# The product with V for two key tiles at once in every second step of an attention block

## The chip, the cores and the metric

One core of one Trainium2 chip. The metric is device time in microseconds (us) for one execution of the whole program, lower is better.

## The reference

One transformer block over X of shape 4 x 1024 x 128 (B = 4 batches, L = 1024 tokens, width 128): a modulated layer norm, attention with 16 heads of 64, and a top-2-of-4 expert layer. The change lies in the attention alone:

```python
qkv = X @ W_qkv + b_qkv                      # b l (H 3 DK) -> Q, K, V of each head
scores = jnp.einsum('bhqd,bhkd->bhqk', Q, K) / np.sqrt(DK)
attn = jax.nn.softmax(scores, axis=-1)
out = jnp.einsum('bhqk,bhkv->bhqv', attn, V) # the product with V
return out.reshape(b, l, H * DK) @ W_fc + b_fc
```

## The kernel before

The attention stage works on pairs of heads: 4 batches x 8 pairs of heads are 32 pairs n, and `run_pairs` issues the first two and the last two with constant indices and the 28 between in a loop of two bodies (u = 0 and 1). A pair is 16 steps s. A step handles one tile of 128 keys (t = s mod 8) against one half of the queries (ch = s div 8, 512 queries), for both heads h of the pair. Keys lie on partitions, so scores, exponentials and the product with V need no transpose.

The engines run their own lists in program order and meet by semaphores.

- **TensorE (PE)**, function `pair`, lines 877 to 899. Each step issues: `scores` (four matmuls, L840 and L841 for each head, full array, 512 columns); `max_half` 0 (L827, scores of a *later* chunk in the other layout, only to find row maxima); a *unit* where the table `UNITS` (line 410) has one; the product with V of the previous step (`v_of_last_step`, then `times_v`, L850); `max_half` 1 (L827). In steps without a unit and with the unit "rows", V stands ahead of the unit, else behind it.
- A call of `times_v` makes, for the two heads, two products of 128 x 64 weights by 512 columns in full fp32. Each is two passes, so it shows as four matmul records. The two heads write the two halves of the partitions of `ps_o` and use the two halves of the array's columns; all other large matmuls of a step use the full array. The unit "sums" (L802) has the same half-array shape.
- The units are: "k", "q", "v" projections of the next pair, "sums" (row sums by a product with ones), "fc" (the output projection), and "rows" (L796: it turns the row maxima into rows, for the next chunk of queries). Steps 0, 2, 4, 6, 8, 10, 14 have k, sums, fc, rows, q, sums, rows; steps 1, 3, 7, 9, 11 have k, q, v, fc, v; steps 5, 12, 13, 15 have none.
- **ScalarE (ACT)** takes the exponentials of both heads (L638, into `PR`, 8 tiles deep), then the copies of its units. **VectorE (DVE)** takes in each step the two reductions of the maxima (L666, one for each `max_half`, in program order), and *behind them* the DVE part of the step's unit: for "rows" the writes of the maxima into `QB` (L689, two of them), for "k" and "q" two subtractions (L677, L682). **GpSimd (POOL)** adds the exponentials up (L581). **SyncE (SP)** moves operands between partitions and spreads the reciprocals.

Waits that the prediction's steps touch:

- `scores` at t = 0 (steps 0 and 8) waits for `neg_rows` (line 834), which the second `QB` write of the unit "rows" of steps 14 and 6 sets.
- `scores` waits for the exponential of the same head of the step before (line 839), `max_half` for the reduction of the same half of the step before (line 825).
- `times_v` waits for the exponentials of its step (line 845); ACT waits for `pv_done` before it overwrites a tile of `PR` that is 8 steps old (line 634). `normalise` (L707) waits for `pv_done` of a whole chunk.

Of the kernel before, what the change touches and what calls it, by code (L numbers as in the profile page):

```python
# [40 lines left out]
def wait(eng, sem, value):  # L41

    if not isinstance(value, int) or value > 0:
        eng.wait_ge(sem, value)
# [285 lines left out]
def attention_stage(nc, g):  # L330
# [7 lines left out]
    NP = B * H // 2  # L338
    PAIRS = H // 2
    SCALE = 0.125  # L340
    with ExitStack() as ctx:
# [56 lines left out]
        def place(s):  # L398

            if s < 6:  # L400
                i = s + 2
                return 0, 1, i // 4, i % 4
            if s < 14:
                i = s - 6
                return 1, 0, i // 4, i % 4
            i = s - 14
            return 1, 1, i // 4, i % 4
# [11 lines left out]
        def unit_at(n, s):  # L419

            if s not in UNITS:
                return None
            kind, d, ch = UNITS[s]
            if isinstance(n, int) and not 0 <= n + d < NP:
                return None
            return kind, n + d, ch
# [4 lines left out]
        def unit_u(s, u):  # L431

            return u if UNITS[s][1] == 0 else 1 - u
# [5 lines left out]
        def has(n):  # L439
            return not isinstance(n, int) or 0 <= n < NP  # L440
# [9 lines left out]
        def half(h):  # L450
            return slice(64 * h, 64 * h + 64)
# [320 lines left out]
        def _(pe):  # L772
# [36 lines left out]
            def freed(kind, m, ch):  # L809

                if kind == "k" or kind == "q":
                    pe.wait_ge(raw_in, raw_count(kind, m, ch))
                else:
                    pe.wait_ge({"v": v_copied, "rows": neg_rows, "sums": sums_in, "fc": fc_added}[kind], 2 * m + ch + 1)

            def max_half(m, u, ch, h, i, kc, count, banks=ps_mx, ahead=0):


                if h == 0 and i == 0 and kc == 0:

                    pe.wait_ge(q_lo, 2 * m + ch + 1)
                    if ch == 0:
                        pe.wait_ge(k_hi, 2 * m + 2)
                        pe.wait_ge(kdup[u], 64 * (m // 2 + 1))
                wait(pe, mx_red, 2 * (count - ahead) - 1 + kc)
                q = ch * 512 + i * P
                T.matmul(banks[:, kc, :], QA[:, u, h, q:q + P], KA[:, u, h, kc * 512:(kc + 1) * 512],  # L827
                         start=True, stop=True).then_inc(mx_done, 1)

            def scores(n, u, s):  # L830
                ch, t = divmod(s, 8)
                q, k = slice(ch * 512, ch * 512 + 512), slice(t * P, (t + 1) * P)
                if t == 0:
                    pe.wait_ge(neg_rows, 2 * n + ch + 1)
                    pe.wait_ge(qdup[u][ch], 32 * (n // 2) + 32)
                    if ch == 0:
                        pe.wait_ge(k_lo, 2 * n + 2)
                for h in range(2):
                    wait(pe, exp_done, 32 * n + 2 * s + h - 1)
                    T.matmul(ps_s[:, h, :], KA[:, u, h, k], QA[:, u, h, q], start=True, stop=False)  # L840
                    T.matmul(ps_s[:, h, :], KB[:, u, h, k], QB[:, u, h, q], start=False, stop=True).then_inc(scored, 1)  # L841

            def times_v(n, u, s):
                ch, t = divmod(s, 8)
                pe.wait_ge(exp_done, 32 * n + 2 * s + 2)
                if t == 0:
                    wait(pe, o_norm, 2 * n + ch - 1)
                    pe.wait_ge(v_copied, 2 * n + 2)
                for h in range(2):
                    last = T.matmul(ps_o[half(h), ch, :], V[:, u, t, half(h)], PR[:, t, h, :], start=(t == 0), stop=(t == 7))  # L850
                last.then_inc(pv_done, 1)
# [15 lines left out]
                freed("q", 0, 1)  # L867
                freed("rows", 0, 0)

            def v_of_last_step(n, u, s):  # L870

                if s > 0:
                    times_v(n, u, s - 1)
                elif has(n - 1):
                    times_v(n - 1, 1 - u, 15)

            def pair(n, u):
                for s in range(16):
                    d, ch, h, i = place(s)
                    grp = (n + d, u if d == 0 else 1 - u, ch, h, i)  # L880
                    scores(n, u, s)
                    if has(n + d):
                        max_half(*grp, 0, 16 * n + s + 10)
                    x = unit_at(n, s)
                    if not x or x[0] == "rows":
                        v_of_last_step(n, u, s)
                    if x:

                        k = ORDER.index(s) - 2
                        before = unit_at(n, ORDER[k]) if k >= 0 else has(n - 1) and unit_at(n - 1, ORDER[k])  # L890
                        if before:
                            freed(*before)
                        if x[0] == "rows":
                            pe.wait_ge(mx_both, 2 * x[1] + x[2] + 1)
                        unit(x[0], x[1], unit_u(s, u), x[2], ps_w2[:, ORDER.index(s) % 2, :])
                    if x and x[0] != "rows":
                        v_of_last_step(n, u, s)
                    if has(n + d):
                        max_half(*grp, 1, 16 * n + s + 10)

            def last():
                times_v(NP - 1, 1, 15)
                freed("fc", NP - 2, 1)
                unit("sums", NP - 1, 1, 1, ps_w2[:, 0, :])
                freed("sums", NP - 1, 0)
                unit("fc", NP - 1, 1, 0, ps_w2[:, 1, :])
                freed("sums", NP - 1, 1)
                unit("fc", NP - 1, 1, 1, ps_w2[:, 0, :])

            run(pe, pair, first, last)  # L910


# [651 lines left out]
```

## Time and profile before

| | |
|---|---|
| median of 3 runs | 1919.35 us (1916.85 to 1920.01) |
| the profiled execution's own time | 1920.44 us |
| its span, first to last instruction | 1918.7 us |
| mean granted TensorE clock | 0.971 |
| PE busy | 1813.9 us (95%) |
| DVE, ACT, POOL busy | 1313.7, 1051.4, 1169.5 us |
| matmuls of the product with V (L850) | 2048 records, 548.9 us |

The attention runs from about 70 us to about 1677 us. In the rows below a line of a timeline gives the start in us from the span's start, the duration in us, the engine and the line. PEld is the weight load that goes ahead of a matmul. Successive matmuls overlap in the records, so the distance between *starts* is what a matmul costs the engine.

### The profile page before, as it was taken

How to read it: one execution, taken by the hardware profiler on the slowest of the kernel's cores; microseconds unless marked ns; L12 is line 12 of the kernel's file. 1: busy time of each engine (PE TensorE's matmuls, PEld its weight loads, DVE VectorE, ACT ScalarE, POOL GpSimd, SP SyncE). 2: the span in 40 equal slices, each digit the busy share in tenths (PEclk: the TensorE clock that was granted, in tenths of full speed). 3: DMA queues.
4: the chain of work that ended last, by engine and by line, in shares of the span. 5: the costliest groups of instructions: out<-in, count | busy, mean ns of one | idle time of the engine just before them, and what ended most of it. 6: DMA issues, size and time to landing. Idle time of an engine off the chain costs nothing. (4 is left out here: it accounts for less than half of the span.)

```text
span 1918.7 us, 29207 instructions
## 1 busy us (share of the span) xinstructions
PE 1813.9 (95%) x7819; PEld 991.3 (52%) x7819; DVE 1313.7 (68%) x2687; ACT 1051.4 (55%) x1944; POOL 1169.5 (61%) x521
## 2 busy tenths in 40 slices
PE   4799999999999999999999999999999999946996
PEld 3444555555555555455555555555555555434886
DVE  5777666666666666666666666666666666467788
ACT  3455555555555555555555555555555555414874
POOL 4466666667666666666766666666667666711124
PEclk8899999999999999999999999999999999956999
DMA  2111111111111111111111111111111111020010
GB/s 84 50 45 50 45 50 47 46 44 50 50 42 41 49 50 50 49 45 43 50 50 50 44 49 48 45 50 47 47 44 50 50 39 40 18 72 22 26 36 28
DMA packets 81217, 87.96 MB, mean 46 GB/s; under 512 B 27773, under 2 KB 50842, under 8 KB 81178
## 3 DMA queue, kind: packets, MB, share of 16 engines
q1 hardware_dynamic: 81024, 87.47, 16.6%
q8 instruction: 18, 0.29, 0.1%
q14 instruction: 21, 0.17, 0.0%
q10 hardware_dynamic: 154, 0.03, 0.0%
HBM read 31.35 MB, written 2.36 MB: 18 GB/s over the span
## 5 line engine op out<-in xcount | busy, mean ns | idle before, releaser
L581 POOL TENSOR_TENSOR ACC<-ACC,PR 128x1024 f32<-128x1024 f32 x382 | 924.6, 2420 | 256.0 <-ACT PR L638 255.1
L666 DVE TENSOR_REDUCE NMH<-ps_mx 128x1 f32<-128x512 f32 x1016 | 693.1, 685 | 491.6 <-PE ps_mx L827 487.1
L638 ACT ACTIVATE PR<-ps_s 128x512 f32<-128x512 f32 x1024 | 556.0, 595 | 617.1 <-PE ps_s L841 612.7
L850 PE MATMUL ps_o<-PR,V 128*64 128x512 f32 x2048 | 548.9, 614 | 0.0
L827 PE MATMUL ps_mx<-KA,QA 128*128 128x512 f32 x1016 | 456.7, 450 | 8.7 <-DVE NMH L666 8.2
L840 PE MATMUL ps_s<-QA,KA 128*128 128x512 f32 x1024 | 408.7, 399 | 0.0
L841 PE MATMUL ps_s<-QB,KB 128*128 128x512 f32 x1024 | 403.4, 394 | 0.0
L827 PEld LDWEIGHTS ps_mx<-KA,QA 128*128 128x128 f32 x1016 | 190.9, 188 | 407.4 <-issue 202.2
L581 POOL TENSOR_TENSOR ACC<-PR 128x1024 f32<-128x1024 f32 x64 | 161.9, 2530 | 278.8 <-ACT PR L638 278.8
L841 PEld LDWEIGHTS ps_s<-QB,KB 128*128 128x128 f32 x1024 | 192.7, 188 | 44.5
L850 PEld LDWEIGHTS ps_o<-PR,V 128*64 128x64 f32 x2048 | 106.9, 135 | 207.2 <-issue 105.0
L840 PEld LDWEIGHTS ps_s<-QA,KA 128*128 128x128 f32 x1024 | 193.2, 189 | 36.0 <-issue 8.1
L609 ACT ACTIVATE raw<-ps_w,bias 128x512 f32<-128x512 f32 x128 | 87.9, 687 | 36.8 <-PE ps_w L785 33.9
L677 DVE TENSOR_TENSOR KB<-raw,KA 64x512 fp32r<-64x512 f32 x128 | 92.9, 726 | 7.5 <-ACT KA L612 5.7
L682 DVE TENSOR_TENSOR QA<-raw,QA 64x512 fp32r<-64x512 f32 x128 | 90.7, 709 | 5.4 <-ACT QA L612 2.6
L689 DVE TENSOR_TENSOR QB<-ps_w,mask 4x512 fp32r<-4x512 f32 x128 | 87.5, 684 | 4.3 <-PE ps_w L796 1.6
L1261 POOL TENSOR_TENSOR e_c<-e_o,e_mv 128x512 f32<-128x512 f32 x7 | 7.3, 1043 | 125.8 <-DVE e_rs L1415 125.8
L612 ACT ACTIVATE KA<-raw 64x512 fp32r<-64x512 f32 x128 | 80.7, 631 | 2.7
L612 ACT ACTIVATE QA<-raw 64x512 fp32r<-64x512 f32 x128 | 80.6, 630 | 2.8
L807 PE MATMUL ps_w<-O,Wfc 128*128 128x512 f32 x128 | 66.4, 601 | 8.4 <-issue 8.4
L791 PEld LDWEIGHTS ps_w<-Wraw,hcur 128*128 128x128 f32 x512 | 66.9, 191 | 7.4 <-ACT raw L609 2.0
L1479 PE MATMUL ps_e<-w2s,e_rT 128*128 128x128 f32 x512 | 63.5, 278 | 6.7 <-DVE e_o L1381 3.4
(187 smaller groups left out, 1519.8 us busy)
## 6 DMA issues: line engine op xcount, KB each, us to landing
hcur<-hT SPq DMA_DIRECT2D x32, 512.0 KB, 3.6
KA<-KA SPq DMA_DIRECT2D x128, 128.0 KB, 2.3
QB<-QA SPq DMA_DIRECT2D x128, 128.0 KB, 2.2
SUM<-recip_rows SPq DMA_DIRECT2D x128, 128.0 KB, 2.9
Wraw<-in_L_attn_W_qkv SPq DMA_DIRECT2D x32, 192.0 KB, 2.4
x<-in_L_attn_X SPq DMA_DIRECT2D x4, 512.0 KB, 5.3
Wfc<-in_L_attn_W_fc SPq DMA_DIRECT2D x32, 64.0 KB, 1.8
R<-SUM SPq DMA_DIRECT2D x128, 2.0 KB, 1.8
```

The lines of the kernel that those rows point to most:

```text
L581: G.tensor_tensor(ACC[:, ch, :, :], a, PR[:, t, :, :], ALU.add).then_inc(added, 1)
L609: A.activation(raw[:, ch, :], ps_w, ACT.Identity, bias=bias[:, u, ty:ty + 1]).then_inc(raw_in, 1)
L612: last = A.activation(X[half(h), u, h, q], raw[half(h), ch, :], ACT.Copy)
L638: A.activation(PR[:, t, h, :], ps_s[:, h, :], ACT.Exp, scale=SCALE).then_inc(exp_done, 1)
L666: D.tensor_reduce(NMH[:, ch, h, i, kc:kc + 1], banks[:, kc, :], AX, ALU.max, negate=True).then_inc(mx_red, 1)
L677: last = D.tensor_tensor(KB[half(h), u, h, q], raw[half(h), ch, :], KA[half(h), u, h, q].bitcast(F32), ALU.subtract)
L682: last = D.tensor_tensor(QA[other(h), u, h, q], raw[half(h), ch, :], QA[half(h), u, h, q].bitcast(F32), ALU.subtract)
L689: last = D.tensor_tensor(QB[top, u, h, q].rearrange("p (i q) -> p i q", i=4), rows, mask[top, :, :], ALU.mult)
L827: T.matmul(banks[:, kc, :], QA[:, u, h, q:q + P], KA[:, u, h, kc * 512:(kc + 1) * 512], start=True, stop=True).then_inc(mx_done, 1)
L840: T.matmul(ps_s[:, h, :], KA[:, u, h, k], QA[:, u, h, q], start=True, stop=False)
L841: T.matmul(ps_s[:, h, :], KB[:, u, h, k], QB[:, u, h, q], start=False, stop=True).then_inc(scored, 1)
L850: last = T.matmul(ps_o[half(h), ch, :], V[:, u, t, half(h)], PR[:, t, h, :], start=(t == 0), stop=(t == 7))
```

## The change

In odd steps PE issues no product with V. In even steps it issues two, for the key tiles of the last two steps, one right behind the other, in the place where the one stood. The last key tile but one of the last pair moves behind the loop, to `last`. The number of matmuls, their shapes and their waits stay as they are; the lists of the other engines are not touched.

```diff
-            def v_of_last_step(n, u, s):
-
+            def v_of_last_steps(n, u, s):
+
+                if s % 2:
+                    return
                 if s > 0:
+                    times_v(n, u, s - 2)
                     times_v(n, u, s - 1)
                 elif has(n - 1):
+                    times_v(n - 1, 1 - u, 14)
                     times_v(n - 1, 1 - u, 15)
...
                     if not x or x[0] == "rows":
-                        v_of_last_step(n, u, s)
+                        v_of_last_steps(n, u, s)
...
                     if x and x[0] != "rows":
-                        v_of_last_step(n, u, s)
+                        v_of_last_steps(n, u, s)
...
             def last():
+                times_v(NP - 1, 1, 14)
                 times_v(NP - 1, 1, 15)
```

## Rows read from the trace of the kernel before

**Rows 1.** Page, part 1: busy time, share of the span and instructions

```profile
PE 1813.9 (95%) x7819; PEld 991.3 (52%) x7819; DVE 1313.7 (68%) x2687; ACT 1051.4 (55%) x1944; POOL 1169.5 (61%) x521
```

**Rows 2.** Windows: length, then busy time of each engine, clock, DMA share, GB/s

```profile
327.00:377.40 50.40, 50.40 (x210) 25.83 (x209) 34.35 (x55) 28.25 (x52) 34.15 (x15) 1.00 0.18 47
...
1700.00:1780.00 80.00, 46.70 (x192) 37.05 (x192) 63.45 (x299) 34.37 (x63) 13.19 (x9) 0.64 0.04 14
```

**Rows 3.** Waits of PEld, 75 to 1600 us: total, times, longest

```profile
PEld ps_s L840 <- issue: 6.2, 28, 0.3
```

**Rows 4.** Timeline of PE, a step without unit (step 12)

```profile
668.36 0.40 PE L840 MATMUL ps_s<-QA,KA 128*128 128x512 f32 x1
...
669.28 0.39 PE L827 MATMUL ps_mx<-KA,QA 128*128 128x512 f32 x1
669.60 1.08 PE L850 MATMUL ps_o<-PR,V 128*64 128x512 f32 x4
670.61 0.50 PE L827 MATMUL ps_mx<-KA,QA 128*128 128x512 f32 x1
670.95 0.39 PE L840 MATMUL ps_s<-QA,KA 128*128 128x512 f32 x1
```

**Rows 5.** Timeline of PE, a step with the unit "sums" (step 10)

```profile
662.34 0.40 PE L827 MATMUL ps_mx<-KA,QA 128*128 128x512 f32 x1
662.67 1.08 PE L802 MATMUL ps_w<-ACC,ones 128*64 128x512 f32 x4
663.58 1.03 PE L850 MATMUL ps_o<-PR,V 128*64 128x512 f32 x4
664.53 0.50 PE L827 MATMUL ps_mx<-KA,QA 128*128 128x512 f32 x1
```

**Rows 6.** Timeline of PE, end of the last pair

```profile
1675.60 1.94 PE L850 MATMUL ps_o<-PR,V 128*64 128x512 f32 x8
```

**Rows 7.** Timeline, from step 14's last matmul into step 0 of the next pair

```profile
676.14 0.50 PE L827 MATMUL ps_mx<-KA,QA 128*128 128x512 f32 x1
...
676.48 0.40 PE L840 MATMUL ps_s<-QA,KA 128*128 128x512 f32 x1
...
676.68 0.69 DVE L666 TENSOR_REDUCE NMH<-ps_mx 128x1 f32<-128x512 f32 x1 [0.81 <-PE ps_mx L827]
...
677.14 1.08 ACT L638 ACTIVATE PR<-ps_s 128x512 f32<-128x512 f32 x2 [1.83 <-PE ps_s L841]
...
677.40 1.38 DVE L689 TENSOR_TENSOR QB<-ps_w,mask 4x512 fp32r<-4x512 f32 x2
...
679.15 0.19 PEld L840 LDWEIGHTS ps_s<-QA,KA 128*128 128x128 f32 x1 [0.23 <-issue]
...
679.49 0.39 PE L841 MATMUL ps_s<-QB,KB 128*128 128x512 f32 x1
```

**Rows 8.** Timeline, the same place where the pair's index is a constant

```profile
1584.14 1.38 DVE L689 TENSOR_TENSOR QB<-ps_w,mask 4x512 fp32r<-4x512 f32 x2
...
1585.58 0.19 PEld L840 LDWEIGHTS ps_s<-QA,KA 128*128 128x128 f32 x1
```

**Rows 9.** Timeline, step 7 (unit "v") after "rows" of step 6

```profile
701.54 0.39 PE L840 MATMUL ps_s<-QA,KA 128*128 128x512 f32 x1
...
702.47 1.38 DVE L689 TENSOR_TENSOR QB<-ps_w,mask 4x512 fp32r<-4x512 f32 x2
...
702.71 1.05 PE L791 MATMUL ps_w<-Wraw,hcur 128*128 128x128 f32 x8
...
703.69 1.08 PE L850 MATMUL ps_o<-PR,V 128*64 128x512 f32 x4
```

**Rows 10.** Page, part 5: subtractions of the unit "k" on DVE

```profile
L677 DVE TENSOR_TENSOR KB<-raw,KA 64x512 fp32r<-64x512 f32 x128 | 92.9, 726 | 7.5 <-ACT KA L612 5.7
```

## The prediction

> **What bounds the kernel now.** I read the page's first part, then windows over single pairs of heads, then the waits of the weight loads, then timelines of single steps. TensorE is busy 1813.9 us of 1918.7 [rows 1]. Over one pair of heads, 50.40 us, it is busy for all of it at a granted clock of 1.00, while DVE works 34.35 us, ACT 28.25 and POOL 34.15 [rows 2]. So in the attention, 32 pairs long, PE's list sets the time, and a start that PE saves is time saved, as long as the next thing that it needs is there. The reader is to look at distances between starts. Four score matmuls start 0.92 us apart in all, 0.23 each [rows 4]. Around the product with V they don't: from the max matmul ahead of it to V 0.32, from V to the next max matmul 1.01, from that to the next score matmul 0.34 [rows 4]. The two 128 x 128 distances of 0.32 and 0.34 in place of 0.23, and the 1.01, of which I will show that only 0.86 is work, are what a change between the full array and the half array costs. One place already has PE waiting: the first score weights of a pair stood idle for 6.2 us in 28 cases [rows 3].
>
> **What a block of V costs, alone and joined.** A step without unit takes 670.95 - 668.36 = 2.59 us [rows 4]. Without V it would be six starts of 0.23, 1.38: an odd step loses 1.21. What does a second V cost right behind the first? The trace has two neighbours of that kind. In the steps with "sums", a half-array product of the same shape stands just ahead of V: from the max matmul to the next one 664.53 - 662.34 = 2.19 [rows 5], against 670.61 - 669.28 = 1.33 with V alone [rows 4]: 0.86 more. At the end of the last pair two V stand together: 1.94 for eight records [rows 6] against 1.08 for four [rows 4], again 0.86. So moving a V from an odd step into an even one costs 0.86 there and saves 1.21 here, 0.35 for each of the 8 couples of steps of a pair of heads, 2.80 us of about 50.4. Over 31 pairs this is 87 us. I take 1.21 for the odd steps with a unit too, an estimate from [rows 4]: V has the same neighbours there, a full-array matmul on both sides. Nothing else is added: no instruction, no DMA, and the lists of DVE, ACT, POOL and SP stay as they are.
>
> **What the moved V had covered.** Odd steps shrink to 1.38 us, or about 2.1 to 2.3 with a unit. What ran beside V there must now be done sooner, or PE waits.
>
> *Step 15 into step 0.* This is the largest term. Score matmuls of step 0 need the maxima written into QB. DVE starts that write behind the last reduction of step 14, which starts 0.54 after step 14's last max matmul (676.14 to 676.68), and it is done at 677.40 + 1.38 = 678.78, 2.30 us after step 15's start at 676.48 [rows 7]. V in step 15 isn't in this chain at all, so its removal doesn't move QB. The first weights of step 0 are loaded at 679.15, 0.37 behind QB; the load had idled 0.23, and the second matmul of the step starts at 679.49, 3.01 after step 15's start [rows 7]. Without any wait it would start at 2.59 + 0.23 = 2.82 before and at 1.38 + 0.23 = 1.61 after. I read the 0.37 as the signal and then PE's own address work for a pair with a variable index: where the index is a constant, the load follows QB's end (1584.14 + 1.38 = 1585.52) by 0.06 [rows 8], and I can't tell there whether it waited. So after the change the second matmul comes at 3.01 again, at the least at 2.30 + 0.06 + 0.34 = 2.70. I take 3.01, since the 28 cases of [rows 3] show the wait where the index varies. The step that gives up a V here gains nothing: 1.21 of the 2.80 are gone, 1.59 are left. (At the other bound 1.90 are left.)
>
> *Step 7 into step 8.* The same wait for QB, written by "rows" of step 6. QB is done at 702.47 + 1.38 = 703.85, 2.31 after step 7's start [rows 9]. Step 7 without V takes 1.17 to its unit (702.71), about 0.9 for the unit (0.98 to V's start, less 0.09 for the change of array), and 0.23 for the last max: 2.3. The second matmul of step 8 would start at 2.53; with the wait it starts at 2.31 + 0.06 to 0.37 + 0.34, that is 2.71 to 3.02. A loss of 0.18 to 0.49. Step 8 has fewer addresses to work out than a new pair, so I take 0.25.
>
> *Reductions that come later.* Step 2's first max matmul needs the first reduction of step 1, which stands on DVE behind step 0's last reduction and behind its unit "k". Counted from step 0's last max matmul: 0.54 + 0.69 [rows 7] + 2 x 0.726 [rows 10] + 0.69 = 3.37. PE gets there after 0.34 + nine starts of step 1 (2.07) + four of step 2 (0.92) = 3.33. The two arrive together. Loss between 0 and 0.2; I take 0.1, and the same for step 6, which stands behind the addition of "fc" in the same way.
>
> *Exponentials.* In a short step without unit both exponentials are done 677.14 + 1.08 - 676.48 = 1.74 after its start [rows 7]. The next step's second head wants its weights at 1.38 + 0.23 = 1.61 and its matmul at 1.84; with 1.74 + 0.06 and 0.1 for the load it starts at 1.90. A loss of 0.05 in steps 6 and 14; step 0 is late anyway.
>
> *Waits that cost nothing.* V waits for exponentials that are now one to two steps old. ACT overwrites a tile of PR 8 steps after it was written, and V of it is issued at the latest two steps after. The last V of each chunk of queries is still issued in steps 8 and 0, so the normalisation, the SP queue's spread of the reciprocals and "fc" see the same order; the cover that hides these is more than a step long.
>
> **The sum.** For one pair: 7 x 1.21 = 8.47 saved in odd steps, 8 x 0.86 = 6.88 spent in even ones, 1.59 left; less 0.25, 0.2 and 0.1, 1.04 us is left. Over 31 pairs that is 32 us. The first pair has no V in step 0 to enlarge, which leaves 0.9 more; the last pair, without max matmuls, I count at nothing. 1920.44 - 33 = 1887 for the profiled execution. The median of the runs is 1.1 below that execution, so I say 1886. Bounds from the terms: all losses at their low end (0.18, 0, 0.1, and 1.90 in place of 1.59) leave 1.62, 50 us, 1869; all at the high end (0.49, 0.4, 0.1) leave 0.60, 19 us, 1901.
>
> **The rivals.**
>
> *The whole saving arrives.* If the 0.37 in [rows 7] is address work alone, and if the QB write moves forward with something that I have overlooked, the sum is 2.80 x 31 = 87 us: 1833. For it: the page gives PE 95%, and no wait of L840 for DVE is listed in [rows 3], only "issue". Against it: QB ends 2.30 after step 15's start and PE's list without V needs 1.38. Chance 0.06.
>
> *No change.* PE waits for DVE as long as V had run. This needs 1.0 us more for a pair than I count, for instance the upper 0.49 in step 8 and 0.2 more in four other steps. About 1919. Chance 0.05.
>
> *Slower, by reductions that never catch up.* In an odd step without unit DVE has two reductions of 0.69, 1.38, and the step lasts no longer. What DVE is late by at the start of an odd step (the units "k", "q", "rows", "fc" stand behind the last reduction, and the longer even step pushes that reduction back) it is late by at its end, and PE's first max matmul of the even step waits. From 1.0 / 8 = 0.13 us at each of the 8 borders beyond what I count this eats the gain; with 0.25 at each, as in step 8, that is 2.0 lost against 1.04, +1.0 for a pair: 1950. Against it: DVE is busy 34.35 of 50.40 [rows 2], so it must be late by place, not by load, and the place that I worked out (step 2) comes out level. Chance 0.08, with 0.02 of it for a granted clock that falls: it was 0.64, a mix of 1.2 and 2.4 GHz, where PE was busy 46.70 us of 80 [rows 2], but here PE stays busy for some 96%.
>
> A page speaks for this rival. The Trainium skill, "TensorEngine Tiling (Array Packing)", section PSUM Bottleneck, says that tiling speeds up TensorE but not the evacuation of PSUM, so that the copy may become the bottleneck. Taken as a bound for the whole it would leave room: an estimate of the DVE-bound pair is DVE's 34.35 us, far below 49. Taken by place it is what I charge in steps 0, 8 and 2, and the trace agrees in step 0. The sum above doesn't use it.
>
> **How the numbers follow.** Forecast 1886, chance 0.81, its own range 1869 to 1901. To hold 8 in 10 with the rivals on both sides the range goes a little beyond: 1860 to 1906. What a measurement can tell from no change is about 0.2%, 4 us. Faster 0.87, same 0.05, slower 0.08.
>
> **What would show it.** In the profile after: even steps without unit take about 3.45 and V stands in blocks of eight records of 1.94; step 13 takes about 1.4; from step 15's start to step 0's second matmul it is still 3.0, with PE idle for over 1 us, and the waits name L840 against DVE QB or "issue" some 31 times with more than 1 us; step 7 takes 2.5 to 2.8; a pair takes about 49.4 in place of 50.4. The prediction is wrong if V's second part costs more than 0.86, if idle PE shows up at the max matmuls of most even steps, or if the wait in step 0 is missing.

## The result, and the profile after

The changed kernel takes 1884.99 us (median of 4 runs, 1884.08 to 1886.73) against 1919.68 before: 0.9823 of it, 95% interval 0.9806 to 0.9840, 34.7 us less. The forecast was 1886. The profiled execution took 1886.73, its span 1885.0.

First the page, part 1 and part 5, to be set against [rows 1]. Columns of part 5: line, engine, operation, out<-in, count | busy, mean ns | idle just before, with what ended most of it.

```profile
PE 1744.5 (93%) x7819; PEld 1009.8 (54%) x7819; DVE 1347.3 (71%) x2687; ACT 1050.9 (56%) x1944; POOL 1172.8 (62%) x521
...
L850 PE MATMUL ps_o<-PR,V 128*64 128x512 f32 x2048 | 494.1, 603 | 0.0
L840 PE MATMUL ps_s<-QA,KA 128*128 128x512 f32 x1024 | 416.0, 406 | 34.9 <-DVE QB L689 34.3
```

PE does the same 7819 matmuls in 69 us less of busy time, and 34.9 us of idle time have come in, all but a little of it ahead of the first score matmul and ended by DVE's QB write. So about half of what the joining freed came out as time. The windows show it over one pair of heads, beside [rows 2]:

```profile
327.00:376.30 49.30, 48.16 (x209) 26.44 (x209) 35.40 (x55) 28.27 (x53) 34.23 (x14) 1.00 0.17 48
```

A pair is about 49.2 us long, PE is busy for 48.16 of 49.30, and the granted clock stays at 1.00. The waits of PE between 75 and 1580 us (total, times, longest) name one place above all (for the second row see the second pair, under what I missed):

```profile
PE ps_s L840 <- DVE QB L689: 33.1, 30, 1.2
PE ps_mx L827 <- DVE NMH L666: 7.4, 6, 2.4
```

And the timeline from step 12 into the next pair, to be read against [rows 4, 7]. Look at the starts of L840 for the steps' ends: step 12 runs from 707.87 to 711.31, step 13 to 712.71, step 14 to 716.54, step 15 to 719.20.

```profile
707.87 0.39 PE L840 MATMUL ps_s<-QA,KA 128*128 128x512 f32 x1
...
709.10 1.94 PE L850 MATMUL ps_o<-PR,V 128*64 128x512 f32 x8
710.97 0.50 PE L827 MATMUL ps_mx<-KA,QA 128*128 128x512 f32 x1
711.31 0.40 PE L840 MATMUL ps_s<-QA,KA 128*128 128x512 f32 x1
...
712.71 0.42 PE L840 MATMUL ps_s<-QA,KA 128*128 128x512 f32 x1
...
716.54 0.39 PE L840 MATMUL ps_s<-QA,KA 128*128 128x512 f32 x1
...
717.47 1.38 DVE L689 TENSOR_TENSOR QB<-ps_w,mask 4x512 fp32r<-4x512 f32 x2
...
719.20 0.49 PE L840 MATMUL ps_s<-QA,KA 128*128 128x512 f32 x1 [1.11 <-DVE QB L689]
719.52 0.40 PE L841 MATMUL ps_s<-QB,KB 128*128 128x512 f32 x1
```

The joined V takes 710.97 - 709.10 = 1.87 to the next start, where one alone took 1.01. Step 12 is 3.44 (2.59 before), step 13 is 1.40 (2.6). In step 15 PE has nothing left to issue after 717.47 + 0.23, stands idle for 1.11, and starts the second matmul of the next pair 719.52 - 716.54 = 2.98 after the step's start, as late as it did before the change (3.01, [rows 7]).

The rest of the document compares steps. The table is worked out from the traces: the distance between the first `L841` of a step and that of the next, the median over the pairs without the first two and the last two, and the length of a pair as the mean of 28.

| step (unit) | before | after | change |
|---|---|---|---|
| 0 (k) | 3.28 | 4.15 | +0.87 |
| 1 (k) | 3.28 | 2.09 | -1.19 |
| 2 (sums) | 3.45 | 4.36 | +0.91 |
| 3 (q) | 3.31 | 2.08 | -1.23 |
| 4 (fc) | 3.46 | 4.31 | +0.85 |
| 5 | 2.59 | 1.42 | -1.17 |
| 6 (rows) | 2.92 | 3.86 | +0.94 |
| 7 (v) | 3.51 | 2.54 | -0.97 |
| 8 (q) | 3.29 | 4.16 | +0.86 |
| 9 (fc) | 3.46 | 2.26 | -1.20 |
| 10 (sums) | 3.46 | 4.31 | +0.86 |
| 11 (v) | 3.49 | 2.28 | -1.21 |
| 12 | 2.59 | 3.46 | +0.87 |
| 13 | 2.61 | 1.42 | -1.19 |
| 14 (rows) | 2.92 | 3.80 | +0.87 |
| 15 | 2.76 | 2.75 | -0.01 |
| one pair | 50.37 | 49.23 | -1.14 |

Every even step pays 0.85 to 0.94, every odd one saves about 1.2, but step 15 saves nothing and step 7 saves 0.24 less.

### The profile page after: what moved, and what is told of

It is laid out like the page before. It is cut to its first block and busy times, and to the rows that moved or that the text cites. A ratio compares the mean times of both kernels' runs of the same rounds, so it can differ in the third digit from the quotient of the medians.

```text
span 1885.0 us, 29221 instructions
## 1 busy us (share of the span) xinstructions
PE 1744.5 (93%) x7819; PEld 1009.8 (54%) x7819; DVE 1347.3 (71%) x2687; ACT 1050.9 (56%) x1944; POOL 1172.8 (62%) x521
## 5 line engine op out<-in xcount | busy, mean ns | idle before, releaser
L666 DVE TENSOR_REDUCE NMH<-ps_mx 128x1 f32<-128x512 f32 x1016 | 678.7, 683 | 377.7 <-PE ps_mx L827 373.0
L850 PE MATMUL ps_o<-PR,V 128*64 128x512 f32 x2048 | 494.1, 603 | 0.0
L840 PE MATMUL ps_s<-QA,KA 128*128 128x512 f32 x1024 | 416.0, 406 | 34.9 <-DVE QB L689 34.3
L827 PE MATMUL ps_mx<-KA,QA 128*128 128x512 f32 x1016 | 436.4, 446 | 11.7 <-DVE NMH L666 11.2
L841 PE MATMUL ps_s<-QB,KB 128*128 128x512 f32 x1024 | 402.8, 393 | 0.0
L581 POOL TENSOR_TENSOR ACC<-PR 128x1024 f32<-128x1024 f32 x64 | 168.9, 2639 | 292.8 <-ACT PR L638 292.8
L850 PEld LDWEIGHTS ps_o<-PR,V 128*64 128x64 f32 x2048 | 130.0, 136 | 261.2 <-issue 187.4
L840 PEld LDWEIGHTS ps_s<-QA,KA 128*128 128x128 f32 x1024 | 192.9, 188 | 116.9 <-ACT PR L638 78.1
L841 PEld LDWEIGHTS ps_s<-QB,KB 128*128 128x128 f32 x1024 | 193.0, 188 | 36.5 <-issue 0.2
L670 DVE TENSOR_TENSOR NM<-NMH 128x8 f32<-128x8 f32 x64 | 93.5, 1461 | 3.5
L689 DVE TENSOR_TENSOR QB<-ps_w,mask 4x512 fp32r<-4x512 f32 x128 | 87.6, 684 | 4.1 <-PE ps_w L796 1.4
L807 PE MATMUL ps_w<-O,Wfc 128*128 128x512 f32 x128 | 66.6, 601 | 8.8 <-issue 8.8
```

The costliest lines, as they stand in the source:

```text
L581: G.tensor_tensor(ACC[:, ch, :, :], a, PR[:, t, :, :], ALU.add).then_inc(added, 1)
L666: D.tensor_reduce(NMH[:, ch, h, i, kc:kc + 1], banks[:, kc, :], AX, ALU.max, negate=True).then_inc(mx_red, 1)
L670: D.tensor_tensor(NM[:, ch, :, :], NMH[:, ch, :, :, 0], NMH[:, ch, :, :, 1], ALU.min).then_inc(mx_both, 1)
```

## The experiments

The theory: joining two V saves 0.35 us by one change of the array less, and the gain is lost again at two places where V had covered DVE's QB write, in step 15 wholly and in step 7 in part. The main rival: a joining is worth 0.35 anywhere, and the rest of the time goes elsewhere, into PE's own address work at the start of a pair for instance. Each experiment is set against the kernel before as it ran beside it: 1919.04 us for the first four, 1913.01 for the next four, 1916.0 (one run) for the last. The second of these is 6 us below the first, so across the groups the length of a pair compares better than the time.

**One joining alone, where nothing is uncovered (e4_only12).** The kernel before, with V of the tiles 10 and 11 joined in step 12. Which tiles a step multiplies stands in a table, and a negative tile is one of the pair before.

```diff
-  if s > 0:
-      times_v(n, u, s - 1)
...
+  V_AT = {0: [-1], 1: [0], 2: [1], 3: [2], 4: [3], 5: [4], 6: [5], 7: [6], 8: [7], 9: [8],
+          10: [9], 12: [10, 11], 13: [12], 14: [13], 15: [14]}
+  for t in V_AT.get(s, ()):
+      if t >= 0:
+          times_v(n, u, t)
+      elif has(n - 1):
+          times_v(n - 1, 1 - u, 16 + t)
```

> The kernel before, with one other part of the change alone: V of tiles 10 and 11 joined in step 12. No wait is uncovered there. Theory: step 11 falls from 3.49 to 2.28, step 12 grows from 2.59 to 3.46; 0.35 us for a pair, 11 us, about 1909 us. Rival (what V costs moves with it, the change of array is free): 0.

1905.38 us against 1919.04, ratio 0.9932 (0.9919 to 0.9946). By the steps: step 11 is 2.28 (3.49 before), step 12 is 3.46 (2.59), the pair 49.99 against 50.37, 0.38 less. The timeline of step 12 is that of the changed kernel. So the price of one change of the array, in and out, stands measured by itself: 0.34 by the two steps (1.21 saved, 0.87 paid) and 0.38 by the pair, as steps 13 to 15 come out 0.04 shorter too. This is in line with [rows 4 to 6].

V differs from its neighbours in two things, the half array and the two records for each product. The unit "fc" (L807) tells them apart: its product also has two records, but uses the full array. Step 9 of the changed kernel, which has "fc" and no V, takes 2.26, that is 0.88 over the 1.38 of six starts. This is what a joined V costs (0.86), without the 0.35, and "fc" starts 0.23 behind the max matmul ahead of it and not 0.32. So the 0.35 goes with the half-array block. In the trace of the changed kernel the loads at its two borders are not made ahead: the first load of the block starts together with its matmul at 709.10, and so does the first load behind it at 710.97, while between full-array matmuls a load starts 0.22 ahead of its matmul (708.56 for 708.78). Whether these loads are the whole cause no run here separates.

**One joining alone, where V is cover (e3_only0).** The kernel before, with V of the tiles 14 and 15 joined in step 0.

```diff
-  if s > 0:
-      times_v(n, u, s - 1)
...
+  V_AT = {0: [-2, -1], 1: [0], 2: [1], 3: [2], 4: [3], 5: [4], 6: [5], 7: [6], 8: [7], 9: [8],
+          10: [9], 11: [10], 12: [11], 13: [12], 14: [13]}
```

> The kernel before, with one part of the change alone: V of tiles 14 and 15 joined in step 0, all others alone as before. Theory: step 15 keeps its 2.77 us, as the QB write holds it, and step 0 takes 0.86 more: 26 us slower than before, about 1945 us. Rival (a joining pays 0.35 us wherever it is): 11 us faster, about 1908 us.

1945.35 us against 1919.04, ratio 1.0132 (1.0117 to 1.0148): the same edit four steps on makes the kernel slower. Step 15 stays at 2.76, step 0 grows to 4.15, the pair to 51.25. PE's waits between 75 and 1560 us:

```profile
PE ps_s L840 <- DVE QB L689: 30.9, 28, 1.2
```

That is the changed kernel's wait, alone. The rival, 1908, falls.

**The change without that one joining (e1_cover15).**

```diff
-  if s % 2:
-      return
...
+  V_AT = {0: [-1], 2: [0, 1], 4: [2, 3], 6: [4, 5], 8: [6, 7], 10: [8, 9], 12: [10, 11], 14: [12, 13], 15: [14]}
```

> The change, but the V of key tile 14 is issued alone in step 15 and that of tile 15 alone in step 0, as before the change; all other couples stay joined. Theory (step 15 needs V as cover for the QB write): step 15 keeps its length of about 2.8 us, since the QB write lasts as long as V, and step 0 loses the 0.86 of the second V: 0.85 us less for a pair, 31 pairs, 26 us less than the changed kernel, about 1859 us. PE's wait of L840 for DVE QB (33.1 us in the changed kernel) falls under 5 us. Rival (every joining pays 0.35 us, nothing is lost at step 15): one joining less, 0.35 more for a pair, about 1896 us.

1860.39 us, ratio 0.9699 (0.9684 to 0.9713). The wait of L840 for QB is gone from PE's waits; the weight load of L840 still shows 0.7 us of it. Step 0 is 3.29, step 15 is 2.76, the pair 48.44, 0.79 under the changed kernel where 0.85 was expected. The missing 0.06 to 0.1 is in step 2 (4.46 in place of 4.36): with step 0 shorter, DVE comes later to step 1's reduction.

**The QB write itself made shorter (e2_half_qb).** V as in the changed kernel.

```diff
-  SCALE = 0.125
+  SCALE = 0.0125
...
   elif kind == "rows":
-      for h in range(2):
+      for h in range(1):
```

> The changed kernel, but the unit rows on DVE writes QB for the first head alone (one write of 0.69 us in place of two); the second head's scores are then not shifted by their maxima, and the scale of the exponentials is a tenth, so that they stay finite. Theory (PE waits for the QB write): it is ready 0.69 us sooner; the wait of step 0 falls by 0.69 us and that of step 8 (0.25) goes: 0.94 for a pair, 29 us, about 1856 us. Rival (PE's own address work for the next pair sets step 0's start): no change, 1885 us.

1855.20 us, ratio 0.9663 (0.9648 to 0.9677), one microsecond from the expected. Step 15 falls from 2.75 to 2.07, by the 0.69 of the write left out, step 7 from 2.54 to its own 2.29. A group of writes that fills 87.6 us of DVE's 1347.3, far down in the page's list, thus costs PE time one for one at the place where PE waits for it. The rival, PE's address work alone, would have left 1885.

**The same without leaving anything out (e5_act_half).** ACT makes the second head's half; below, ACT's unit, DVE's unit, and PE's further wait in `scores` (it has the same one where the unit's bank is freed).

```diff
+  elif kind == "rows":
+      act.wait_ge(rows_t, 2 * m + ch + 1)
+      for i in range(4):
+          last = A.activation(QB[0:4, u, 1, ch * 512 + i * P:ch * 512 + (i + 1) * P], ps_w[0:4, P:2 * P],
+                              ACT.Copy, scale=mask[0:4, i, 0:1])
+      last.then_inc(neg_rows_b, 1)
...
-      for h in range(2):
+      for h in range(1):
...
+  pe.wait_ge(neg_rows_b, 2 * n + ch + 1)
```

> The changed kernel with the same result, but the second head's QB write of the unit rows is made by ACT, as four copies of 4 x 128 with the mask's column as scale, and DVE makes the first head's alone; PE waits for both. Theory (step 0 and step 8 wait for the QB writes): ACT is idle there and is done ahead of DVE, so the write is complete 0.69 us sooner, as in the run that left the second write out: about 1855 us. Rival (the writes only moved): the copies on ACT or the further wait on PE take as long, 1885 us.

1854.11 us against 1913.01, ratio 0.9686 (0.9652 to 0.9720); the pair is 48.25, that of the run before. The timeline around step 15, which starts at 703.45:

```profile
703.23 1.11 ACT L621 ACTIVATE QB<-ps_w,mask 4x128 fp32r<-4x128 f32 x4 [1.83 <-PE ps_w L805]
...
704.37 0.69 DVE L698 TENSOR_TENSOR QB<-ps_w,mask 4x512 fp32r<-4x512 f32 x1
...
705.39 0.19 PEld L852 LDWEIGHTS ps_s<-QA,KA 128*128 128x128 f32 x1 [0.82 <-ACT PR L647]
```

ACT is done at 704.34, before DVE has begun its half at 704.37; the write is complete at 705.06, 1.61 after the step's start and not 2.31. The load follows 0.33 later. (The profile puts the wait down to an exponential here; the first head's was long done.)

**Both repairs (e6_act_half_cover).** The table of e1_cover15 and the ACT half of e5_act_half.

> Both repairs together: V of tile 14 alone in step 15 and that of tile 15 alone in step 0, and ACT makes half of the QB writes. Theory: step 15 is V's own 2.6 us with no wait left, step 7 its own 2.29: 0.42 less for a pair than with V in step 15 alone (1860), 13 us: about 1847 us. Rival (the two repairs remove the same wait, nothing is left for the second but the price of one joining, 0.35): 1855 + 11 = 1866 us.

1847.36 us, ratio 0.9650 (0.9617 to 0.9683): the fastest kernel of this study, under both the kernel before and the changed one. Step 15 is V's own 2.59 in all pairs, step 7 is 2.28, the pair 48.01. The longest of PE's waits between 75 and 1560 us:

```profile
PE ps_mx L838 <- DVE NMH L675: 7.5, 6, 2.4
...
```

The other two of the list are single waits, of 0.4 and 0.3 us. No wait that repeats in each pair is left in it.

**Four tiles at once (e8_quads).**

```diff
-  if s % 2:
-      return
...
+  V_AT = {0: [-4, -3, -2, -1], 4: [0, 1, 2, 3], 8: [4, 5, 6, 7], 12: [8, 9, 10, 11]}
```

> The change taken further: V of four key tiles at once, in steps 0, 4, 8 and 12 alone. Theory: four joinings more save 1.4 us for a pair, but rows in steps 6 and 14 now waits for NM with no V ahead of it, about 2 us each, and step 15 has no cover either: 2.6 us more for a pair than the changed kernel, about 1965 us. Rival (a joining pays 0.35 wherever it is): 1842 us.

2015.72 us against 1913.01, ratio 1.0524 (1.0481 to 1.0567): the direction was right, the size was not, by 50 us. PE's waits between 75 and 1560 us:

```profile
PE ps_w L796 <- DVE NM L670: 89.7, 55, 1.7
PE ps_s L840 <- DVE QB L689: 22.0, 20, 1.2
PE ps_mx L827 <- DVE NMH L666: 20.2, 33, 2.4
```

By steps the pair is 53.45, 4.22 over the changed kernel. Steps 6 and 14 take 3.68 each, where the same step without V would take 2.92 - 1.21 = 1.71: 1.97 lost twice, as expected. What I had miscounted: steps 2 and 10 still change the array for "sums" (step 10 is 2.60, which is 4.31 less two times 0.86), so two changes are saved and not four, 0.70 and not 1.4. And steps 2 and 3 (2.75 and 2.91, against 2.60 and 2.08) wait 0.98 for reductions that come late. 3.94 - 0.70 + 0.98 = 4.22; the medians of the steps add up to 4.12, so these terms are good to 0.1. Eight of the 28 pairs also hold a stretch of 3.4 us at a granted clock of 0.50 (502.0 to 505.4 is the first), behind one of the idle stretches of 1.67 or 1.68 us that PE has in steps 6 and 14; these pairs are 0.2 to 0.3 longer than the shortest ones.

This is not the slower rival as the prediction had it. That one had max matmuls wait for late reductions, which are 20.2 us here; the bulk, 89.7 us, is the wait of "rows" for NM, DVE's minimum of the maxima, with which the next runs deal. In one step 14 PE stood idle for 1.68 us (at 768.74) behind an NM that took 1.61, where 0.17 is NM's own time in the last run below. So 1.44 of the 1.68 would go with what holds NM; this is an estimate from these figures, as no run took both edits.

**What holds NM (e7_short_add, e9_short_add5).** In the trace after, DVE's minimum of the maxima, NM, had grown to twice its time or more, though nothing of DVE was edited. One line of before and its neighbour on POOL:

```profile
672.85 2.39 POOL L581 TENSOR_TENSOR ACC<-ACC,PR 128x1024 f32<-128x1024 f32 x1 [0.21 <-ACT PR L638]
...
674.48 0.79 DVE L670 TENSOR_TENSOR NM<-NMH 128x8 f32<-128x8 f32 x1
```

POOL ends at 675.24, NM at 675.27. So the two runs shorten one of POOL's additions, which costs the row sums a tile: that of tile 4, in the second run that of tile 5. The scale is 0.0125 in both, as in e2_half_qb.

```diff
-  G.tensor_tensor(ACC[:, ch, :, :], a, PR[:, t, :, :], ALU.add).then_inc(added, 1)
+  if t == 4:
+      G.tensor_tensor(ACC[:, ch, :, 0:8], ACC[:, ch, :, 0:8], PR[:, t, :, 0:8], ALU.add).then_inc(added, 1)
+  else:
+      G.tensor_tensor(ACC[:, ch, :, :], a, PR[:, t, :, :], ALU.add).then_inc(added, 1)
```

> The changed kernel, but POOL adds only 8 of 512 columns at key tile 4 of each chunk (the row sums then lack most of that tile), and the exponentials' scale is a tenth. Theory on the longer NM (it lasted 0.7 to 0.8 us before the change, 1.3 to 1.6 after, and ends 0.02 us behind POOL's addition every time): DVE's small operation is held until POOL's addition ends, so NM falls to about 0.2 us. Rival (NM waits for its own reductions or for a semaphore): it stays at 1.3 to 1.6. The time as a whole moves by less than 3 us, as V covers NM in steps 6 and 14.

The first missed its mark: tile 4's addition is over by the time NM is due, tile 5's runs then. NM stayed at 1.48 us, and the run (1879.18 us, a single one) tells nothing for or against.

> As the run before with a short addition, at the right tile: POOL adds only 8 of 512 columns at key tile 5 of each chunk, the addition that runs while NM is due (at tile 4 it was over by then); the row sums lack most of that tile and the exponentials' scale is a tenth. Theory (DVE's NM, with two operands in SBUF, is held until POOL's addition ends): NM falls from 1.48 us to about 0.2. Rival (NM waits for its own reductions or a semaphore): it stays at 1.48. The time moves by less than 3 us, as V covers NM.

All 64 NM of the kernel after, by the view of one line (count: shortest/median/longest in ns, first and last start in us):

```profile
L670 DVE TENSOR_TENSOR NM<-NMH x64: 167/1560/2045, 65.7 to 1622.9; 128x8 f32<-128x8 f32 x64
```

and of this run:

```profile
L673 DVE TENSOR_TENSOR NM<-NMH x64: 166/168/169, 65.3 to 1621.2; 128x8 f32<-128x8 f32 x64
```

With the addition out of the way NM takes 0.17 us, every time. The traces before and after say the same: an addition was running when NM started in 61 of 64 cases before and in 62 after, and each of these NM ended 0.02 to 0.03 us behind that addition; the other five took 0.17. The time is 1882.59 us (one run, against 1916.0), and the pair is 49.23, as in the changed kernel: V covers NM there, and nothing was to be gained.

## Why the prediction was right, point by point

**The price of V, alone and joined**: 1.21 and 0.86 were read off two neighbours in the trace [rows 4 to 6]. The odd steps without a wait save 1.17 to 1.23, the even ones pay 0.85 to 0.87 where nothing else happens, and one joining by itself gave 0.38 for a pair where 0.35 was said.

**Step 15**: said to gain nothing, for the QB write isn't moved by V's removal. It takes 2.75 in place of 2.76. The removal and the restoring of V there (e3_only0, e1_cover15) and the shorter write (e2_half_qb) show the cause. This term decided the forecast: without it, it would have been 1848.

**The 0.37 behind QB**: I could not tell signal from address work, and kept both bounds. The trace after can, since PE now waits in both cases. Where the pair's index is a constant the load comes 0.05 after the write's end; where it varies, 0.34 after (717.47 + 1.38 = 718.85, load at 719.19).

```profile
1554.50 1.38 DVE L689 TENSOR_TENSOR QB<-ps_w,mask 4x512 fp32r<-4x512 f32 x2
...
1555.93 0.19 PEld L840 LDWEIGHTS ps_s<-QA,KA 128*128 128x128 f32 x1 [1.22 <-DVE QB L689]
```

What lies between stands in the traces. In each of the 28 pairs of the loop PE's queue runs three operations there, at L835, L837 and L44, the first and the last of them always register work; in the pair of [rows 7] they start 0.04, 0.17 and 0.27 behind the write's end, and the load 0.37 behind it. In the pairs with constant indices none stands there. By the view of the line L835, before:

```profile
L835 PEldq FUSED_REGOPS  x28: 42/60/97, 174.9 to 1535.2; - x28
```

So some 0.3 us is address work that starts only behind the wait, and the value taken (3.01) was the right end. The queue could have told this before the change: its work starts 0.04 behind the write there too, so QB held step 15 already then, which is why it took 2.76 and not V's own 2.59.

**Step 7 into step 8**: said 0.25, between 0.18 and 0.49. It is 2.54 - 2.28 = 0.26 by the runs in which the write is short. Here the write ends at 694.63 and the load comes at 694.76, 0.13 later, and one register operation stands between (694.67), so a step in the middle of a pair has less address work behind the wait, as assumed.

**Late reductions** in steps 2 and 6 were 0.05 and 0.08 and not 0.1 each; **late exponentials** ahead of steps 6 and 14 were 0.03 each and not 0.05. One reason is in step 2's chain: I took the two subtractions at 0.726 each, a mean over both units "k" [rows 10]; those of step 0, which stand in this chain, take 1.38 or 1.39 together in every pair. These small terms were over-sized by 0.11 together, which with the rounding of 1.21 and 0.86 makes 1.14 for a pair out of the 1.04 that I summed.

**The total**: that it came within 1 us of the forecast is in part luck. The profiled executions differ by 33.7. The 28 pairs of the loop give 32.1 of it, where 28 times 1.04 is 29.1. The second pair got 3.5 longer, where I had counted a gain; the last got 0.6 longer, the first 0.5 and the last but one 1.2 shorter. And 4.1 come from ahead of and behind the attention, where nothing was changed: from the last matmul of "fc" (L807) to the end it is 229.0 before and 225.6 after, and it runs from 223.3 to 230.7 over the eleven traces.

**The rivals**: the whole saving (1833) failed at step 15. No change falls by the interval (0.9806 to 0.9840). The slower one, by late reductions, did not come about in the loop: max matmuls wait 7.4 us in all, 4.6 of them in the second pair. The clock, part of that rival, is 1.00 in the attention from 75 us on, before, and after as well but for one stretch in the second pair.

**What I missed**: that NM would grow. It starts sooner behind a short step and then waits longer for the end of POOL's addition; V in steps 6 and 14 hid it. Without V ahead of "rows" PE waits for it, as in e8_quads.

I also missed the second pair. A DVE operation that comes once (L756, 2.75 us) stands ahead of a reduction there. In step 10 PE stood idle for 2.39 us for it, and just behind that the granted clock fell to 0.50, the lower of its two levels (1.2 GHz):

```profile
159.80:163.20 3.40, 3.40 (x10) 0.73 (x6) 0.63 (x2) 1.29 (x5) 0.46 (x1) 0.50 0.03 5
```

The joined V took 3.33 in place of 1.94 there, and the step 8.66 in place of 4.93 before. In the six experiments that also join V in step 10 and in which the clock stayed at 1.00 at this place it takes 6.97 to 6.99, so about 1.7 of it goes with the clock. My sum had the same terms for all pairs and none for this.

## What to carry to other kernels

Joining half-array matmuls saved 0.34 to 0.38 us for each change of the array that went, and a trace of the kernel before can show that price if two such matmuls already stand together somewhere. Before a piece of the bounding engine's work is moved, list for the place that it leaves which waits of other engines it had covered, and count from when that engine could start: a chain that does not contain the moved work does not get shorter by its removal. Where one such place gives the gain back, leave that one piece where it was (0.79 us of a pair of 49.23 here), or shorten the chain by handing half of it to an idle engine (0.98); both together gave 1.22.

## What the runs showed of the hardware that I had not expected

A DVE operation on 128 x 8 elements, both operands in SBUF, took 0.17 us by itself and up to 2.05 us beside POOL's additions on SBUF operands, and ended 0.02 to 0.03 us behind the addition in every case in which one was running at its start, before and after. The reductions from PSUM beside it kept their 0.69. So the hold lasts until the addition ends, and it shows as duration of the DVE operation and not as idle time. The Trainium skill, "SBUF — State Buffer", section Who interferes with whom, says that a DVE instruction with two SBUF inputs contends with a GpSimd instruction that reads SBUF, and that the order of issue decides which of the two is blocked; these traces agree, with the numbers given.

The first weight load of a pair comes 0.05 us behind the write that it waits for where addresses are constants, and 0.34 or 0.37 us behind it in the loop, where three operations of PE's queue, register work among them, run between. Here address work that stands behind a wait was not hidden by the wait.

The price of a block of half-array matmuls among full-array ones, 0.34 to 0.38 us, shows at its borders, where the weight loads start together with their matmuls and not 0.22 us ahead.
